# Local attention: 64-row transposes, scores in quarters of the array without masked key blocks, copies out of PSUM shared anew, a new order on every engine

## The reference

```python
qkv = x @ Wqkv                       # 128 -> 3 x 1024: q, k, v of 16 heads x 64
q = l2norm(q) * qs ; k = l2norm(k) * ksc
q = q * cos * scale + rotate_half(q) * sin * scale     # k alike, with 1/scale
# query i of window w (32 tokens) sees the keys of windows w-1 and w
mask = (it < jb) | (it > jb + w) | (jb == -1)
sim = where(mask, -max, einsum(q, k) * 8)
out = einsum(softmax(sim), v)
x = out @ Wo + x                     # then layer norm and gated FFN
```

## Time and profile before

| | |
|---|---|
| three runs | 5235.75, 5230.54, 5233.23 us, median 5233.23 |
| the profiled execution | 5234.16 us, its span on the core 5232.4 us |
| granted TensorE clock, mean | 0.943 |
| busy share | PE 89%, PEld 59%, DVE 70%, ACT 75%, POOL 61% |

### The profile page before, as it was taken

The page is one execution under the profiler, slowest core; times in us unless marked ns, Lnnn a source line. Parts: engine busy times, 40 slices in busy tenths (PEclk is TensorE's granted clock), DMA queues, the critical chain, the costliest instruction groups (busy, mean ns, idle before and its releaser), DMA issues. The chain is left out here.

```text
span 5232.4 us, 127320 instructions
## 1 busy us (share of the span) xinstructions
PE 4669.1 (89%) x37624; PEld 3090.5 (59%) x37626; DVE 3672.2 (70%) x8669; ACT 3902.5 (75%) x13654; POOL 3202.0 (61%) x4057
## 2 busy tenths in 40 slices
PE   6859899998999989999899989999899997667775
PEld 3436566665666656666566655666566664444443
DVE  4779777755777467774677737787377773777578
ACT  6948788865888668885688847888488883777434
POOL 2412588855888468884788837888288882332153
PEclk9969999999999999999999999999999998888887
DMA  1000000000000000000000000000000000000000
GB/s 53 1 18 0 6 1 0 0 17 6 1 0 0 17 6 1 0 0 17 7 0 0 0 21 3 0 0 0 22 2 0 0 1 18 1 0 0 1 25 17
DMA packets 36285, 34.21 MB, mean 7 GB/s; under 512 B 11574, under 2 KB 31156, under 8 KB 34996
## 3 DMA queue, kind: packets, MB, share of 16 engines
q1 hardware_dynamic: 36020, 31.06, 2.1%
HBM read 28.95 MB, written 2.10 MB: 6 GB/s over the span
## 5 line engine op out<-in xcount | busy, mean ns | idle before, releaser
L2447 ACT ACTIVATE local_prob<-ps,local_shift_by 128x128 f32<-128x128 f32 x3072 | 1083.9, 380 | 35.5 <-DVE local_shift_by L2551 23.3
L2400 POOL TENSOR_TENSOR local_qk<-local_qk,local_inv 128x512 f32<-128x512 f32 x768 | 792.2, 1043 | 343.6 <-ACT local_inv L2487 343.6
L2393 POOL TENSOR_TENSOR local_qk<-local_qk,local_rsin 128x512 f32<-128x512 f32 x768 | 961.1, 1272 | 49.8 <-DVE local_rsin L2576 49.8
L2565 DVE TENSOR_TENSOR local_qk<-ps,local_cos_t 128x512 f32<-128x512 f32 x768 | 530.6, 691 | 643.6 <-ACT local_sq L2470 631.0
L2407 POOL TENSOR_TENSOR local_prob<-local_prob,local_rs 128x512 f32<-128x512 f32 x768 | 791.0, 1040 | 195.1 <-DVE local_rs L2558 195.0
L2681 PE MATMUL ps<-local_wqkv,local_xsT 128*128 128x512 f32 x1536 | 826.8, 625 | 29.4 <-DVE local_rsin L2576 25.2
L2447 ACT ACTIVATION_READ_ACCUMULATOR local_prob<-ps,local_shift_by 128x1 f32 x3072 | 676.2, 220 | 0.0
L2470 ACT ACTIVATE local_sq<-ps 128x512 f32<-128x512 f32 x768 | 472.8, 616 | 194.3 <-PE ps L2681 148.9
L2576 DVE TENSOR_TENSOR local_rsin<-ps,local_sin_t 128x256 f32<-128x256 f32 x1536 | 567.6, 410 | 0.0
L2551 DVE TENSOR_REDUCE local_shift_by<-ps 128x4 f32<-128x512 f32 x768 | 503.6, 677 | 56.7 <-PE ps L2722 53.4
L2583 DVE TENSOR_REDUCE local_ss<-local_sq 128x8 f32<-128x512 f32 x768 | 500.4, 673 | 0.0
(11 more groups left out here) (326 smaller groups left out, 9071.1 us busy)
## 6 DMA issues: line engine op xcount, KB each, us to landing
local_wqkv<-L_ffn_Wqkv SPq DMA_DIRECT2D x7, 1536.0 KB, 6.5
local_wo<-L_ffn_Wo SPq DMA_DIRECT2D x7, 512.0 KB, 7.2
out<-quantised_res SPq DMA_DIRECT2D x8, 256.0 KB, 2.3
local_w<-L_ffn_W SPq DMA_DIRECT2D x6, 341.0 KB
L_cross_decay<-c_decay SPq DMA_DIRECT2D x1, 1024.0 KB, 11.6
local_w<-L_ffn_W SPq DMA_DIRECT2D x12, 64.0 KB
load_raw<-L_ffn_w SPq DMA_DIRECT2D x8, 64.0 KB, 2.1
local_b<-L_ffn_b SPq DMA_DIRECT2D x24, 0.5 KB
```

Source lines behind the costliest of these rows:

```text
L2393: nc.gpsimd.tensor_tensor(qk[w][:, j, :, :], qk[w][:, j, :, :], rsin[j % 2][:, :, :], ALU.add).then_inc(rot_ready, 1)
L2400: nc.gpsimd.tensor_tensor(qk[w][:, j, :, :], qk[w][:, j, :, :], bcast(inv[:, w, 8 * j:8 * j + 8].unsqueeze(2), [P, 8, LH]), ALU.mult).then ...
L2447: last = nc.scalar.activation(prob[w][:, g, j, :], ps[:, 4 + g % 2, j * P:(j + 1) * P], ACT.Exp, bias=shift_by[:, w, h:h + 1], accum_out=s ...
L2565: nc.vector.tensor_tensor(qk[w][:, j, :, :], bank, bcast(cos_t[:, j // 2, :].unsqueeze(1), [P, 8, LH]), ALU.mult)
```

## The change

It touches `local_attention` and the constants that it reads.

- **Transposes in row halves.** `turn_qk` and `turn_probs` are now two groups a batch each. A group takes 16 transposes of 64 rows x 128 columns: tokens 0 to 63 on rows 0 to 63 of the array into bank 2, tokens 64 to 127 on rows 64 to 127 into bank 3. Both kinds use both banks, 2 and 3.
- **Scores in quarters.** Masks and products are split by queries as well: queries 0 to 63 with keys 0 to 63, queries 64 to 127 with keys 32 to 127. Each is a matmul on 64 rows and 64 columns of the array. The blocks left out keep the -1e30 that two matmuls at the start of the phase write there.
- **Copies out of PSUM.** A group's two banks are copied by one instruction each. For q and k ACT takes bank 2 and DVE bank 3, for probabilities ACT takes both, values go half by DVE and half by ACT, heads half by ACT and half by DVE. A batch has 12 such copies of 128x512 before and after. Before, ACT did 11 and DVE 1; now ACT does 8 and DVE 4.
- **Order and waits.** Every `step` is written in another order. Inside the loop PE leaves out waits that others imply, and `waits_alone` puts four waits ahead of a transpose group or of scores. There are 13 more semaphores, one more constant table to load and to convert at the start.

```diff
-            def turn_qk(b, w, j, live):
...
-                    for c in range(4):
-                        last = nc.tensor.transpose(ps[:, 3, c * P:(c + 1) * P],
-                                                   qk[w][:, j, 2 * c:2 * c + 2, :].rearrange("p h e -> p (h e)"), ident[:, :])
+            def turn_qk(b, w, half, live):
+                if live(b):
+                    if half == 0:
+                        waits_alone(pe, env, (unit_ready[half], b + 1), (unit_ready[2 + half], b + 1),
+                                    (probT_ready[0][0], b - 1), (probT_ready[0][1], b - 1))
...
+                    for i in range(2):
+                        for c in range(4):
+                            for p in range(2):
+                                r = slice(LH * p, LH * p + LH)
+                                last = nc.tensor.transpose(ps[:, 2 + p, (4 * i + c) * LH:(4 * i + c) * LH + LH],
+                                                           qk[w][r, 2 * i + half, 2 * c:2 * c + 2, :].rearrange("p h e -> p (h e)"),
+                                                           ident[r, r])
...
             def scores(b, w, half, live):
...
-                    for p in range(2):
-                        wait(pe, exp_ready, 4 * b + 2 * half + p - 1)
-                        nc.tensor.matmul(ps[:, 4 + p, :].rearrange("p (h k) -> p h k", h=HG), identb[:, :],
-                                         bcast(band[:, :].unsqueeze(1), [P, HG, P]), start=True, stop=False)
-                    for j in range(HG):
+                    for keys, part in ((HALF_KEYS[0], slice(0, LH)), (HALF_KEYS[1], slice(LH, P))):
                         for p in range(2):
                             r = slice(LH * p, LH * p + LH)
-                            last = nc.tensor.matmul(ps[:, 4 + p, j * P:(j + 1) * P], qkT[w][r, half, j, :],
-                                                    qkT[w][r, 2 + half, j, :], start=False, stop=j == HG - 1)
...
+                            many = keys.stop - keys.start
+                            at = 0 if part.start == 0 else LH
+                            nc.tensor.matmul(ps[part, 4 + p, :].rearrange("q (h k) -> q h k", h=HG)[:, :, keys], identb[r, r],
+                                             bcast(env["band2"][r, at:at + many].unsqueeze(1), [LH, HG, many]), start=True, stop=False)
                     for j in range(HG):
...
+                        for keys, part in ((HALF_KEYS[0], slice(0, LH)), (HALF_KEYS[1], slice(LH, P))):
+                            for p in range(2):
+                                r = slice(LH * p, LH * p + LH)
+                                last = nc.tensor.matmul(ps[part, 4 + p, j * P + keys.start:j * P + keys.stop], qkT[w][r, half, 0, j, part],
+                                                        qkT[w][r, half, 1, j, keys], start=False, stop=j == HG - 1)
...
+            def evacuate_qk(b, w, half, p, live):
+                if live(b):
+                    dve.wait_ge(qk_turned, 2 * b + half + 1)
+                    nc.vector.tensor_copy(qkT[w][:, half, :, :, LH * p:LH * p + LH],
+                                          ps[:, 2 + p, :].rearrange("p (i c t) -> p i c t", i=2, c=4)).then_inc(qkT_ready[half][p], 1)
...
             def step(n, u, live):
                 v = 1 - u
-                shift(n - 3, v, live)
-                turn_probs(n - 1, v, 0, live)
...
-            sequence_loop(pe, NB, 2, 3, step)
+                turn_qk(n - 2, u, 0, live)
+                output(n - 5, v, live)
...
+            sequence_loop(pe, NB, 0, 5, step)
```

More of the change, by code:

```diff
@@ L57, in wait_alone, with waits_alone @@
     eng.wait_ge(sem, value)
+def waits_alone(eng, env, *pairs):
+    if all(isinstance(value, int) for _, value in pairs):
+        for sem, value in pairs:
+            wait(eng, sem, value)
+        return
+    pairs = [(sem, eng.to_reg(value)) for sem, value in pairs]
+    eng.wait_ge(env["made"], 1)
+    for sem, value in pairs:
+        eng.wait_ge(sem, value)
 def sequence_loop(eng, count, lead, lag, step):
@@ L2644, in step @@
[L2644 to L2648 removed]
+                maxima(n - 1, v, 0, live)
+                evacuate_qk(n - 1, v, 1, 1, live)
+                evacuate_values(n - 1, v, 0, live)
+                bound_norms(n, u, live)
+                maxima(n - 1, v, 1, live)
+                one_over_sums(n - 2, u, 2, live)
@@ new lines, in step @@
+                maxima(n - 1, v, 2, live)
+                one_over_sums(n - 1, v, 1, live)
+                evacuate_qk(n, u, 0, 1, live)
+                maxima(n - 1, v, 3, live)
+                sums_of_squares(n + 1, v, 2, live)
+                residual(n - 3, v, live)
+                norm(n - 5, v, live)
+                cosines(n + 1, v, 2, live)
+                sines(n + 1, v, 2, live)
+                cosines(n + 1, v, 3, live)
+                sines(n + 1, v, 3, live)
+                sums_of_squares(n + 1, v, 3, live)
@@ L2650, in _ @@
+            sequence_loop(dve, NB, 1, 5, step)
         @block.tensor
@@ new lines, in scores @@
+                    for j in range(HG):
+                        for keys, part in ((HALF_KEYS[0], slice(0, LH)), (HALF_KEYS[1], slice(LH, P))):
+                            for p in range(2):
+                                r = slice(LH * p, LH * p + LH)
+                                last = nc.tensor.matmul(ps[part, 4 + p, j * P + keys.start:j * P + keys.stop], qkT[w][r, half, 0, j, part],
+                                                        qkT[w][r, half, 1, j, keys], start=False, stop=j == HG - 1)
+                                if j == HG - 1 and part.stop == P:
+                                    last.then_inc(scores_ready, 1)
```

367 lines of the change are left out of this document (209 added, 158 removed).

## The result

The changed kernel takes 4976.66 us, median of 4 runs (4972.15 to 4977.98), against 5232.39 us: a ratio of 0.9509, 95% interval 0.9493 to 0.9526. Forecast were 4895 us, a ratio of 0.936. So 257 us came where 338 were expected; the range of 4820 to 5095 holds the time. Its profiled execution has a span of 4973.7 us. One execution of experiment 4's kernel, the profiled one, took 8190 us where its other four took 4897 to 4905, so its trace isn't used.

What follows compares the result with a forecast made beforehand. PE's own list was taken as the bound, 16.66 us a period. From 5234.2 us, six layers of 27 x (16.66 - 14.7) + 5 take 347 off, 6 come on: 4893, forecast as 4895, range 4820 to 5095.

Steps and rivals of the forecast that it cites:

- PE's list, 14.44 us: PE's work in one steady period of local attention, changes of shape included: 14.44 us, 2.22 less than before.
- 0.084: Time in us of a PE score slot of four quarters, set by its longest, 96 of 128 columns; 16 slots, 1.34.
- Rivals 2 and 3: On PE: tiles overlap less, 5077 or 5164 us, chance 0.13; or short matmuls' loads aren't hidden, 5335 us, chance 0.06.
- Changes of shape, 11 x 0.17: PE changes the array shape in use 11 times a batch, for 8, at 0.17 us each: 1.87 us, a loss of 0.38.
- the forecast's 1.63: PE's gain a period from transposes on row halves: 32 pairs at 0.058 us, 1.86 for 3.49.
- DVE's 14.6 and 0.3 us of waits: DVE's list with three more copies takes 14.6 us a period; waits between engines add 0.3, making the period 14.7.
- The cycle: Tightest place: DVE's second sines free PE's bank for `project` 2, then scores, then DVE's third maxima; 14.5 us round.
- Filling and emptying, 5 us less a layer: At both ends of each layer's pipeline, one step longer but with shorter steps: 5 us less, 0 to 8.
- Rival 1: Waits between four nearly full engines make the period 15.3 to 16.2 us, time 4996 to 5148; chance 0.22.
- Rivals 4 and 5: A hidden hand-over holds the old period, 5230 us, chance 0.03; or period 14.1 to 14.4, 4795 to 4844, chance 0.06.
- rival 2: On PE, tiles overlap less: quarters only in pairs, period 15.8 us, or row halves not at all, 16.3; chance 0.13.

Runs made afterwards that it cites:

- experiment 4: Changed kernel with `bound_norms` (maximum of 32 sums a partition and 1e-24) moved one place down DVE's list, behind the second maxima: 4900.27 us, ratio 0.9372.
- experiment 1: Changed kernel without `bound_norms`; ACT's logarithm waits for the sums itself and adds 1e-18 to 2^20 times the sum: 4876.77 us, ratio 0.9328.
- experiment 3: Changed kernel with POOL's rotation of the last quarter of q and k cut to one of eight heads, for timing alone: 4876.37 us, ratio 0.9330.
- Experiments 1 to 3: Changed kernel, three separate edits: `bound_norms` removed, 4876.77 us; written as `tensor_reduce` in the same place, 4872.72; POOL's last rotation cut short, 4876.37.
- Experiment 8: Changed kernel with transposes, masks and scores as in the kernel before, leaving new order, copy shares and semaphores: 5259.41 us, ratio 1.0053.
- experiment 9: Changed kernel without `bound_norms`, with three of DVE's four copies out of PSUM given back to ACT: 5044.89 us, ratio 0.9647.
- experiment 12: Kernel before with only masks and scores in quarters, old order, transposes and copies kept; start mask matmuls left out: 5063.61 us, ratio 0.9687.

## Why the prediction was right, and where it was off

By its own steps, one after the other:

- **PE's list, 14.44 us: right as a sum, its parts less so.** Freed of waits it is 14.46. Transposes with their change of shape 0.64 (0.46 + 0.17 forecast). Masks and scores 0.95 a half, where 0.17 + 0.67 + 0.17 were forecast. But a slot of the scores is 0.10 and not 0.084, some 0.27 us a period more, and cheaper masks and changes of shape gave that back. That the sum fits to 0.02 us is in part luck. Rivals 2 and 3, with 0.19 together, are refuted by the timeline.
- **Changes of shape, 11 x 0.17: no single price.** Undoing the row halves costs 0.86 a period; that would be 0.19 for each of the four that go, if the streaming gains the forecast's 1.63 (1.63 - 0.86 = 0.77), which no run separates. Adding one costs 0.10, measured.
- **DVE's 14.6 and 0.3 us of waits: this step failed.** The cycle was the right one. Its parts were forecast as 12.1 + 0.86 + 1.3 + 0.2. In the timeline above `project` 2 to third maxima takes 2.11 us (1938.59 to 1940.70; forecast 0.86 + 1.3 = 2.16), and the third maxima to the end of the second sines 13.06 (to 1953.02 + 0.74; forecast 12.1); in every other period this second stretch is 12.72. In experiment 1 it is 12.26 and 12.09 in turn, as forecast. So what was forecast too short is the place of `bound_norms`, which the prediction doesn't name and which keeps DVE for 1.04 us here (1949.40 to 1950.44), for 0.87 in the period ahead (1934.34 to 1935.21), and for 0.08 where nothing holds it (1944.37 to 1944.45 in experiment 3). Experiments 1 to 3 show it: without its wait PE's list is the bound. It cost 15.04 - 14.46 = 0.58 us a period, 162 x 0.58 = 94 of the measured 100 us. The forecast had allowed 14.7 - 14.44 = 0.26 as waits; the period is 15.04 - 14.7 = 0.34 above it, and 0.34 x 162 = 55 us is two thirds of the miss.
- **The trace of before had the sign.** In the period of the earlier trace rows `bound_norms` takes 0.21 us, in the next one 1.27, and over the whole kernel it is:

```profile
L2588 DVE TENSOR_SCALAR local_ss<-local_ss 128x32 f32<-128x32 f32 x192 | 128.0, 667 | 6.6
```

A mean of 667 ns for 32 elements should have made me ask. And a second `tensor_scalar` from SBUF to SBUF stood in the period of the earlier trace rows itself, the layer norm's, DVE's row and POOL's of the same time:

```profile
2008.64 1.00 DVE L2617 TENSOR_SCALAR XN<-local_xs,local_moments,local_rstd 128x128 f32 x1
2008.52 1.05 POOL L2400 TENSOR_TENSOR local_qk<-local_qk,local_inv 128x512 f32<-128x512 f32 x1
```

Of the 192 instances of this line 156 start while a GpSimd instruction runs, and all of these end 80 to 88 ns after it; the other 36 last 314 to 348 ns. Of `bound_norms` in the changed kernel the view over the whole kernel says:

```profile
L2594 DVE TENSOR_SCALAR local_ss<-local_ss 128x32 f32<-128x32 f32 x192 | 177.5, 924 | 0.2
```

- **Filling and emptying, 5 us less a layer: wrong.** A layer's phase went from 555.5 to 510.7 us, 44.8 less, and 27 x 1.62 of it, 43.7, is the steady part: 1 us was gained, not 5. That is 24 us, the rest of the miss (55 + 24 = 79 of 82). Experiment 8 gives the size without the tiles: 7 us a layer are lost at the ends, and PE idles there for 21 us in the changed kernel where it was 15. I had named the longer pipeline ("a batch leaves one step later") and let the shorter steps outweigh it. What I left out is the clock: in the first window of a layer it is 0.77 where it was 0.83 (the earlier trace rows and the rows above). Which of the two costs how much isn't shown.
- **Rival 1** (waits between four nearly full engines) is what happened in kind: period 15.04 lies between the forecast's 14.7 and its 15.3, inside the 14.4 to 15.1 that I had given the forecast. The cover that the two tile changes together needed was the new shares of the copies (experiment 9).
- **Rivals 4 and 5** are out by the period: 15.04 is neither 16.6 nor 14.1 to 14.4, and even freed of waits it is 14.46.
- **A slip in the rivals' times.** By the formula of the forecast, 5234.2 - 6 x (27 x (16.66 - period) + 5) + 6, rival 1's periods of 15.3 and 16.2 give 4990 and 5136 us, and rival 2's 15.8 and 16.3 give 5071 and 5152. The prediction has 4996 and 5148, 5077 and 5164, and a middle of 5045 for rival 1 that isn't the middle of its range. No verdict hangs on these 6 to 12 us.

## What to carry to other kernels

When a change makes the leading engine faster, price the next engine's list from a view over many periods, and ask of each instruction that takes longer than its elements explain what it stands behind: a stall counted as busy time is free until that engine enters the cycle. A VectorE `tensor_scalar` from SBUF to SBUF beside a busy GpSimd is such a place, the `tensor_reduce` here isn't; another form or one place further down the list can be all that is needed. Then test the steady period and the ends of the pipeline apart, and read the granted clock of the ends too: here the new order gained nothing in the steady stretch by itself and cost 7 us a layer outside it.

## What the runs showed of the hardware that I had not expected

- A VectorE `tensor_scalar` on 128x32 float32, SBUF to SBUF, lasts 171 ns when GpSimd's instruction ends at once, and 0.95 to 1.12 us beside a 1.27 us GpSimd instruction, whose end it waits for (it ends 35 to 43 ns after it, 180 times of 180); a `tensor_reduce` of 128x64 in its place lasts 208 ns beside the same instructions. A `tensor_scalar` on 128x128 in the kernel before, 314 to 348 ns beside an idle GpSimd, lasts up to 1.01 us beside a busy one and ends 80 to 88 ns after it.
- Row and column halves together run four float32 matmuls side by side: 32 of 64 to 96 columns in 0.81 us, 25 ns each, and with 128 columns 30 ns each.
- The price of a change of the array's shape is not one number: 0.10 us where a single transpose was set between two other shapes; the group behind sixteen half transposes takes 0.96 us, behind eight whole ones 0.86.
- The granted clock in the first 50 us of a layer differed with the order of the kernel: 0.87 in the mean of six layers with the old order (kernel before, experiment 12), 0.78 to 0.82 with the new one (changed kernel, experiments 1 and 8). Single layers overlap (0.82 to 0.92 and 0.73 to 0.88).
